# Causal masks by selects on GpSimd and transfers on the sync queue in a two-layer transformer forward pass

## What is computed

```python
# layer 0: 16 heads of 64, each key/value head serves 4 query heads
scores = einsum('bhqd,bhkd->bhqk', q, k) * 64 ** -0.5
scores = scores + triu(full((S, S), -inf), k=1)
out = einsum('bhqk,bhkd->bhqd', softmax(scores, axis=-1), v)
return out.transpose(0, 2, 1, 3).reshape(B, S, 1024) @ Wo.T
# layer 1's block: the same with heads of 8, and where(causal, scores, -inf)
```

## Time and profile before

| | |
|---|---|
| runs | 1661.58, 1665.15, 1666.9 us |
| profiled execution, its own time | 1658.08 us |
| its span | 1656.2 us |
| busy over the span | PE 82%, weight loads 50%, DVE 64%, ACT 40%, POOL 10% |
| mean granted TensorE clock | 0.886 of full speed |
| layer 0's attention | 43.5 to 733 us of the span |
| second attention | 1146 to 1447 us of the span |

### The profile page before, as it was taken

One profiled execution on the slowest core, in us unless ns is written; L12 is line 12 of the kernel. 1 busy time (PEld: TensorE's weight loads), 2 busy tenths in 40 slices (PEclk: granted clock), 3 DMA queues, 4 the chain that ended last, 5 costly groups with the idle time before them and its releaser, 6 DMA issues. The chain is left out here.

```text
span 1656.2 us, 20400 instructions
## 1 busy us (share of the span) xinstructions
PE 1353.3 (82%) x6684; PEld 821.3 (50%) x6684; DVE 1066.6 (64%) x1626; ACT 654.4 (40%) x1176; POOL 161.5 (10%) x189
## 2 busy tenths in 40 slices
PE   3789999999999999922999995541799988469996
PEld 3345454555555555412777774430444443146875
DVE  4645455555646463246899996682767777057997
ACT  1132323333323333302555553320266666425663
POOL 0100101010100000000111110021011111101110
PEclk9679999999999999965999997865589999868997
DMA  2000101010101101011666650007012220203220
GB/s 82 5 9 1 32 1 35 9 26 9 26 9 25 28 6 30 1 30 45 143 138 150 143 124 1 0 1 203 1 44 51 63 60 18 59 2 115 86 80 26
DMA packets 40351, 79.29 MB, mean 48 GB/s; under 512 B 11376, under 2 KB 29688, under 8 KB 35576
## 3 DMA queue, kind: packets, MB, share of 16 engines
q1 hardware_dynamic: 39136, 69.82, 16.8%
q0 software_dynamic: 1152, 8.65, 2.5%
HBM read 69.47 MB, written 8.45 MB: 47 GB/s over the span
## 5 line engine op out<-in xcount | busy, mean ns | idle before, releaser
L584 ACT ACTIVATE shared<-ps 128x1024 f32<-128x1024 f32 (+7 forms) x256 | 166.0, 651 | 409.1 <-PE ps L430 252.9
L446 PE MATMUL ps<-shared,Vg 128*65 128x512 f32 (+3 forms) x768 | 295.2, 494 | 7.3 <-ACT shared L584 4.3
L497 DVE TENSOR_REDUCE mraw<-ps 128x1 f32<-128x512 f32 (+3 forms) x304 | 196.8, 660 | 114.0 <-PE ps L397 85.9
L1226 PE MATMUL ps<-qA 128*128 128x512 f32 x960 | 255.1, 402 | 18.2 <-DVE qA L1338 13.2
L904 DVE TENSOR_REDUCE mraw<-ps 128x2 f32<-128x1024 f32 (+3 forms) x160 | 174.4, 1115 | 86.1 <-PE ps L824 62.6
L1226 PEld LDWEIGHTS ps<-qA 128*128 128x128 f32 x960 | 178.5, 191 | 75.9 <-DVE shared L1351 17.7
L948 ACT ACTIVATE shared<-ps 128x512 f32<-128x512 f32 (+2 forms) x320 | 154.0, 563 | 124.8 <-PE ps L840 124.6
L393 PE MATMUL ps<-kH,qA 128*128 128x512 f32 (+3 forms) x384 | 185.9, 514 | 17.0 <-DVE mraw L497 13.2
L428 PE MATMUL ps<-qA,kH 128*128 128x512 f32 (+3 forms) x384 | 190.7, 497 | 2.7 <-DMA qB<-mT 2.7
L1280 ACT CAST qA<-shared 128x512 fp32r<-128x512 f32 x160 | 99.4, 621 | 135.1 <-DVE shared L1358 134.6
L1237 PE MATMUL ps<-qA,kH 128*128 128x512 f32 x480 | 136.3, 393 | 4.3 <-DVE qA L1332 4.3
(11 more groups left out here) (255 smaller groups left out, 1665.6 us busy)
## 6 DMA issues: line engine op xcount, KB each, us to landing
shared<-comb SPq DMA_DIRECT2D x96, 256.0 KB, 4.5
rB<-a0rec_dram POOLq DMA_DIRECT2D x8, 1024.0 KB, 7.0
shared<-comb SPq DMA_DIRECT2D x8, 1024.0 KB, 4.5
q_split<-qA SPq DMA_DIRECT2D x8, 512.0 KB
qA<-q_split SPq DMA_DIRECT2D x16, 256.0 KB, 4.1
rB<-a1rec_dram SPq DMA_DIRECT2D x32, 128.0 KB, 2.7
e0wUp<-in_w SPq DMA_DIRECT2D x48, 64.0 KB, 4.6
wqk<-in_wqk SPq DMA_DIRECT2D x8, 192.0 KB, 2.4
```

Of the source, the lines that this page charges most:

```text
L446: ins = nc.tensor.matmul(O[0:65, lo:hi], k.Vg[par][:, kt, :], k.PT[:, slot % PTR, lo:hi], start=(kt == 0), stop=(kt == 4 * ch + 3))
L497: ins = nc.vector.tensor_reduce(out, bank[:, 0:n_h * width].rearrange("p (h w) -> p h w", w=width), AX, ALU.max)
L584: nc.scalar.activation(k.PT[:, slot % PTR, kt * P:S], score_banks(slot)[:, kt * P:S], ACT.Exp, scale=scale).then_inc(p_full, 1)
L1226: ins = nc.tensor.matmul(bank[0:M, :], w[par][:, at:at + M], h[:, cols], start=(r == 0), stop=(r == 2))
```

## The change

In layer 0's attention the mask matmul of `scores` goes. POOL instead sets the masked part of the diagonal block in `PT` to zero after the exponential, one `affine_select` of 128x128 per slot, 256 in all, and `values` waits for it (`masked`) ahead of its lowest chunk, taking the upper chunk first. The cast of q into `qB` becomes a transfer from SBUF to SBUF. It, the gathering of the sums and the spreading of the reciprocals move to SP's queue; both POOL's and SP's loops are written out. In the jobs of the maxima of both attentions the masks of heads that share a bank are one wider matmul, whose moving operand repeats the tile.

```diff
 # fill, kind "max"
-                                               ..., start=True, stop=not diagonal)
-                        if diagonal:
-                            ins = nc.tensor.matmul(bank[:, (j + 1) * width - P:(j + 1) * width], k.ident_bf[:, :],
-                                                   k.masks[:, 1, :], start=False, stop=True)
+                                               ..., start=(j == 0), stop=not diagonal,
+                                               skip_group_check=True)
+                    if diagonal:
+                        ends = bank[:, 0:n_h * width].rearrange("p (h w) -> p h w", w=width)[:, :, width - P:width]
+                        ins = nc.tensor.matmul(ends, k.ident_bf[:, :],
+                                               k.masks[:, 1:2, :].broadcast_to((P, n_h, P)), start=False, stop=True,
+                                               skip_group_check=True)
 # scores
-                    pe.wait_ge(qb_done, g + 1)
+                    pe.wait_ge(qb_ld[par], 16 * (half + 1))
...
-                    if diagonal:
-                        ins = nc.tensor.matmul(region[:, lo:lo + P], k.ident_bf[:, :], k.masks[:, 0, :],
-                                               start=False, stop=True)
 # values
-                for ch in range(kt // 4, CPB):
+                for ch in range(CPB - 1, kt // 4 - 1, -1):
+                    if ch == kt // 4:
+                        pe.wait_ge(masked, NSLOT * g + slot + 1)
                     if kt == 0:
                         pe.wait_ge(oU_full, CPB * (REP * g + h) + ch + 1)
 # gpsimd (qB's cast, gather_sums and spread leave it)
+            prep_v(0)
+            for g in range(G):
+                for slot in range(NSLOT):
+                    kt = slot % TPB
+                    pool.wait_ge(p_full, NSLOT * g + slot + 3)
+                    tile = k.PT[:, slot % PTR, kt * P:(kt + 1) * P]
+                    nc.gpsimd.affine_select(tile, tile, [[1, P]], ALU.is_ge, 0.0, base=0,
+                                            channel_multiplier=-1).then_inc(masked, 1)
+                    if slot == 2 and g + 1 < G:
+                        prep_v(g + 1)
 # sync
+            def copy_q(group):
+
+                sp.wait_ge(q_hi, NPROJ * (group + 1))
+                sp.dma_start(k.qB[group % 2][0:hd, :, :].bitcast(F32), k.qA[group % 2][0:hd, :, :].bitcast(F32))\
+                    .then_inc(qb_ld[group % 2], 16)
...
+            load(0)
+            copy_q(0)
             rows(0, NPREP - 1)
             load_wo(0)
+            for g in range(G):
+                if g + 1 < G:
+                    load(g + 1)
+                if g:
+                    gather_sums(g)
+                    spread(g)
+                if g + 1 < G:
+                    copy_q(g + 1)
+                    rows(g + 1, base(g) + NPREP - 1)
+                if g:
+                    sp.wait_ge(w_free, base(g) + (LAST_FIN + 3 if g + 1 < G else NFIN - 1 + 3))
+                    load_wo(g // B)
+            gather_sums(G)
+            spread(G)
 # stage_attention8, max_job
-                        for slot in range(len(js)):
-                            for part in range(2):
-                                for i in range(2):
...
+                        for part in range(2):
+                            for i in range(2):
+                                rows = row_tile(i, 64)
+                                ends = pair[:, i, 0:n_j * w].rearrange("p (j w) -> p j w", w=w)[:, :, w - P:w]
+                                ins = nc.tensor.matmul(ends, k.halves[rows, 0, part, :],
+                                                       k.halves[rows, 1, part:part + 1, :].broadcast_to((64, n_j, P)),
+                                                       start=False, stop=(part == 1), skip_group_check=True)
```

More of the change, by code:

```diff
@@ L598, in _, with prep_v @@
         def _(pool):
[L599 to L601 removed]
+            def prep_v(group):
+                kv, par = divmod(group, B)
+                if group >= 2:
                     pool.wait_ge(pt_free, heads(REP * (group - 1)))
[L603 removed]
                 nc.gpsimd.tensor_copy(k.Vg[par][:, :, 0:hd], k.V[:, par * TPB:(par + 1) * TPB,
[L605 to L608, removed]
@@ L643, in _, with load @@
         @block.sync
         def _(sp):
-            def load(group, par, kv):
-                if not (isinstance(group, int) and group < 2):
+            def load(group):
+                kv, par = divmod(group, B)
+                if group >= 2:
                     sp.wait_ge(q_hi, NPROJ * (group - 1))
-                sp.dma_start(k.wqk[:, par, :], wqk[bass.ds(kv, 1)].rearrange("o p n -> (o p) n"))\
-                    .then_inc(in_ld[par], 16)
-            def rows(par, last):
-                row = k.qB[par][hd:hd + 1, :, :].bitcast(F32).rearrange("o h q -> o (h q)")
+                sp.dma_start(k.wqk[:, par, :], wqk[kv]).then_inc(in_ld[par], 16)
@@ L655, in rows @@
+            def copy_q(group):
+                sp.wait_ge(q_hi, NPROJ * (group + 1))
+                sp.dma_start(k.qB[group % 2][0:hd, :, :].bitcast(F32), k.qA[group % 2][0:hd, :, :].bitcast(F32))\
+                    .then_inc(qb_ld[group % 2], 16)
+            def rows(group, last):
+                row = k.qB[group % 2][hd:hd + 1, :, :].bitcast(F32).rearrange("o h q -> o (h q)")
                 for i in range(2):
@@ L819, in max_job @@
                     if diagonal:
-                        for slot in range(len(js)):
-                            for part in range(2):
-                                for i in range(2):
-                                    rows = row_tile(i, 64)
-                                    ins = nc.tensor.matmul(pair[:, i, (slot + 1) * w - P:(slot + 1) * w],
-                                                           k.halves[rows, 0, part, :], k.halves[rows, 1, part, :],
-                                                           start=False, stop=(part == 1), skip_group_check=True)
+                        n_j = len(js)
+                        for part in range(2):
[5 more added lines that the diff above has]
+                                                       start=False, stop=(part == 1), skip_group_check=True)
                     ins.then_inc(x_full, 1)
```

65 lines of the change are left out of this document (18 added, 47 removed).

## The result

The changed kernel takes 1612.8 us (median of 4 runs, 1611.12 to 1615.38) where the kernel before, measured beside it, takes 1665.9 us (4 runs, 1661.58 to 1666.9). The ratio is 0.970, with a 95% interval of 0.9666 to 0.9729. The prediction was 1616 us. The profiled execution took 1614.19 us, its span is 1612.5 us.

The account below looks back on a forecast made before the run. PE was taken to bound layer 0's attention. Gains of 23 + 3 + 23 + 6 less costs of 3.6 and 3 gave 48.4 us, taking the profiled 1658.1 to 1610, or 1616 us on the median's scale; range 1600 to 1641 us.

Parts of the forecast that it names:

- the stop in slots 5 to 7, with the clock: Groups 1 to 6: without POOL's cast beside DVE's normalisation, PE's 1.95 us stop and the lower clock go; gain 23 us.
- masks of the scores, selects, extra wait: Layer 0's slots: removing 256 mask matmuls gains 23 us; uncovered selects cost 3.6 us, one more PE wait 3 us.
- masks of the maxima: Layer 0's maxima jobs: joining masks of heads into wider matmuls, 32 to 22 per group, gains 3 us.
- transfers (two chains): Last group's start and stage's end: transfer chains DVE waits for get shorter on SP's queue; gain 3 us each.
- second attention: Its maxima masks become 384 instead of 512 with all columns kept; taken as 0 us.
- signs named: Profile rows that would show the forecast right, among them broadcast landing in 4.5 to 7 us, end chain near 10 us.
- Rival 1: Slots 5 to 7: PE's stop or the lower clock stays, 23 us of gain missing; 1639 us, chance 0.2.
- The extra wait: PE's stream, every slot: one more wait, priced like a mask's issue, 0.04 us; loss 3 us.
- The order of the chunks: Values at key tile 0: upper bank, copied last, is needed first; nothing, or 0.2 us x 32 where DVE is late.
- rival 2: Normalisations on DVE and selects on POOL exclude each other at a shared port; 6 us lost, 1622 us, chance 0.13.
- rival 3: The select paces PE, deciding from 1.8 us after the exponential; 1713 us at 2.1 us, chance 0.06.
- rival 4: DVE's and ACT's waits absorb PE's savings, or masks cost nothing; gains of 0 to 5 us, 1663 us, chance 0.03.

Follow-up runs that it names:

- experiment 3: Against the kernel before: the sums' and reciprocals' transfers on SP's queue, all masks still on PE, q still cast on POOL; 1658.1 us, 0.995.
- experiment 2: The changed kernel with all masks back on PE, no selects, values in the old order, transfers on SP's queue and q copied by transfer; 1631.2 us, 0.980.
- 7: The changed kernel with the masks of layer 0's maxima narrow again, 256 instead of 176; 1617.8 us, 0.975.
- experiment 9: The changed kernel with one more, already met wait per slot in PE's stream ahead of the values of layer 0's attention; 1618.0 us, 0.972.
- experiment 1: The changed kernel with the second attention's masks narrow again, 512 instead of 384; 1616.2 us, 0.970.
- 4: The changed kernel with a pause on DVE, eight memsets, ahead of the second attention; 1618.1 us, 0.973.
- 5: The changed kernel with each select done twice per slot, the second changing nothing; 1622.7 us, 0.979.

## Why the prediction was right, and where its terms were off

Three kernels between before and after (3, 2 and 7) split the stage's 51.4 us in the order of the prediction's terms:

| term | predicted, us | measured, us | from |
|---|---|---|---|
| the stop in slots 5 to 7, with the clock | -23 | -23.3 | 3 to 2 |
| masks of the scores, selects, extra wait | -23 + 3.6 + 3 | -17.3 (14.7 in the steady groups) | 2 to 7 |
| masks of the maxima | -3 | -3.3 (1.8 in the steady groups) | 7 to after |
| transfers (two chains) | -6 | -7.5 (4.4 in the chains) | before to 3 |
| sum, layer 0's attention | -48.4 | -51.4 | |
| second attention | 0 | +6.6 in the profiled execution | |

The prediction's own figures add up to 1617 us, not 1616. The sum was right also by some luck: 1.6 us in group 6, 1.7 us in the last group and about 2 us in group 0 are shorter stretches at half clock that no term had. Of the signs named, two were missed: the broadcast landed in 7.2 us, outside 4.5 to 7, and the end chain took 11.6 us, not 10.

**The stop** came out by its own steps: normalisation 1.22 us, PE's wait for the reduction 0.2 us per group where 0.4 was left to it, no window at 0.50. Rival 1 (the stop stays) is out: experiment 3 has the stop with the cast and 2 has none without it, and the kernel after has none although PE waits longer in slot 5.

**The masks of the scores** are net 17.3 us where 16.4 were expected, but the terms inside were distributed otherwise. The selects' waits cost 8.5 us of PE where the exponential's had cost 4.3 in experiment 2: 4.2 us, for 3.6 predicted, and they are where the prediction had them, in slot 5 of seven groups and in the very last slot. The latency taken as 0.4 us is about 0.5: 0.07 us from the exponential's end to the select, 0.29 us of select (predicted 0.30), 0.15 us to PE (the select at 255.74 ends at 256.03, PE starts at 256.18); slot 5 shows it as 1.13 - 0.61 = 0.52 us. **The extra wait was the term mis-sized**: 3 us were taken from the nearest row, the issue of a mask, and experiment 9 shows 0.4 us; a mask's issue was no measure of a wait's. The order of the chunks was costed at nothing as a loss; it is a gain that the prediction's cover ("the upper chunk goes first, which holds PE some 0.9 us") needed: without it the stage is 9.7 us longer.

**The masks of the maxima** were taken as 3 us and are worth 1.8; the 3.3 us of the table agree with the forecast only through group 0's clock.

**The chains** gave 2.8 and 1.6 us, for 3 and 3. The step that failed was the price of the broadcast. The 4.5 us of another 1 MB load from SP's queue were the better bound and 7.0 us the worse, and the worse one held: 7.2 us. The gain is in the other steps: a shorter store (1.4 for 1.7 us), and SP's queue issues 0.03 us after what it waits for, POOL's 0.6 us. The Trainium skill ("DMA: Bandwidth & Descriptors", "Latency and other measured facts") gives the sync queue about 0.4 us less to the first byte than GpSimd's; the store shows 0.3 us of that here, the broadcast (7.0 to 7.2 us) and the gathering (2.3 to 2.4 us) nothing.

**The port** (rival 2) exists and was overpriced. 14 selects started during a normalisation, not 32, and six of them (slot 14) near its end, which cost 0.04 us each. Held long were 8: slot 27 of six groups (1.02 us each; PE waited for none of them) and slots 16 and 24 of the last group (1.10 and 1.22 us). Getting these two out of the way gave 0.7 us in the last group, for an expected price of 6.

**Slower** (rival 3) needed a latency of 1.8 us. It is 0.5, and a second select costs 10 us, so that even this kernel is far below the one before. **No change** (rival 4) fell with the 17 us from experiment 2 to 7.

**The second attention** was taken as 0, and its masks are 0 (experiment 1). What the prediction did not have is that a stage outside the change may get another clock that its own change doesn't explain (experiments 1 and 4). In the profiled execution this takes 6.6 us; without it the execution would stand at 1607.6 us, against 1610 predicted on that scale, so here the 3 us gained beyond the sum are outweighed. How often the kernel before meets the lower clock there in its other runs stays open: only profiled executions show it. The medians hint that it mostly does: of the five profiled executions at full clock there, four (before and experiments 2, 3 and 5) are 6 to 9 us below their kernel's median, the pause's is at it; those at the lower clock are 2.5 us below to 5.9 us above theirs.

## What to carry to other kernels

Before an elementwise pass is moved to GpSimd or off it, look at which VectorE instruction runs beside it and what is queued behind that one: here one cast of 3.6 us, off every critical path by itself, cost 23 us through a normalisation and the clock. A mask by a select after the exponential costs little where the matmul that needs the masked block can be put last (here 4.2 us of PE's waits against the 17 us of net gain), and 8 to 10 us more where it goes first. A broadcast that feeds one head at a time should land one head at a time: here that took 3.7 us off the wait at the stage's end, and the other queue 1.6 us off the same chain, none of it in the broadcast. And a difference of some us in a stage that nobody changed is a reason to look at its clock first.

## What the runs showed of the hardware

- The same instructions of a sparse part ran at a granted clock of 1.00 (from 1372.5 us on, with a pause ahead of the stage) and of 0.50 (from 1365.5 us on, without), behind 20 us that were equally busy (17.4 us): 12.3 or 18.9 us. What decides is not shown.
- A select of 128x128 on GpSimd takes 0.29 us alone and up to 1.22 us when it starts during a VectorE multiplication of two SBUF inputs, always ending about 0.15 us after it. The other way round, the multiplication ends 1.07 us after the select or cast that was running when it began: 3.38 us for 1.22 beside a cast of 3.60.
- 32 waits of TensorE that are already met cost 0.05 us at most, within what groups differ by.
- A mask matmul of 128 bf16 columns starts the next one 0.04 us later, but the 512-column pair behind it is 0.32 us apart instead of 0.24.
- GpSimd's queue began a transfer 0.6 us after what it waited for, SyncE's 0.03 us after.
- 1 MB spread over 64 partitions from DRAM lands in 7.2 us; in four parts, 5.0 us each, it let DVE start 3.7 us sooner.
